# Expert layers with a table of tokens by slot, and feed-forward stages with routed tiles between halves of the shared expert

## The reference, cut to what matters

```python
# L0_ffn: 8 experts, two per token, inner width 512
probs = softmax(30 * tanh((x @ w_gate) / 30)); mask = one_hot(top_k(probs, 2)).sum(-2)
out = sum_e (silu(x @ w1[e]) * (x @ w3[e])) @ w2[e] * (probs * mask)[:, e]
# L1_ffn, second part: 8 routed experts of width 176, two per token, and a shared one of width 704
h = rms(x) * w_ln2;  probs = softmax(h @ w_router);  combine = the two largest probs, 0 elsewhere
routed = sum_e combine[:, e] * (silu(h @ w_gate_e[e]) * (h @ w_up_e[e])) @ w_down_e[e]
sh = (silu(h @ w_sh_gate) * (h @ w_sh_up)) @ w_sh_down * sigmoid(h @ w_sh_eg)
x = x + routed + sh
```

## Time and profile before

| | |
|---|---|
| Time, median of 3 runs | 2636.81 us (2633.54 to 2636.89) |
| Profiled execution | 2635.1 us, its span 2633.0 us |
| Instructions | 45240 |
| PE busy | 2078.7 us (79%), mean granted clock 0.857 |
| DVE, ACT, POOL busy | 1525.1 (58%), 1180.3 (45%), 1044.7 us (40%) |
| DMA | 179.47 MB, mean 68 GB/s |

### The profile page before, as it was taken

How to read it: one execution, slowest core, us unless ns; L and a number is a source line. 1 busy time by engine, 2 the same in 40 slices (tenths; PEclk the granted TensorE clock), 3 DMA queues, 4 the chain that set the end, 5 groups by cost and what they waited for, 6 DMA issues and landing times. The chain is left out here.

```text
span 2633.0 us, 45240 instructions
## 1 busy us (share of the span) xinstructions
PE 2078.7 (79%) x16876; PEld 1605.9 (61%) x16888; DVE 1525.1 (58%) x3266; ACT 1180.3 (45%) x2905; POOL 1044.7 (40%) x965
## 2 busy tenths in 40 slices
PE   8497438978887995967798577976789676779798
PEld 5365225646565874756587466865668665546686
DVE  2222642236675335787876876868778678357432
ACT  3211421126364333853566545655556555236433
POOL 0222012220002542586535864368623767100254
PEclk9698768989998997967799588996789777989799
DMA  8422013210003303321322213222122221120430
GB/s 288 132 24 48 9 39 71 25 44 2 23 2 97 142 0 70 106 73 33 113 80 78 69 50 100 89 63 81 57 89 81 67 69 65 37 55 2 126 113 16
DMA packets 138317, 179.47 MB, mean 68 GB/s; under 512 B 62048, under 2 KB 114544, under 8 KB 132992
## 3 DMA queue, kind: packets, MB, share of 16 engines
q1 hardware_dynamic: 129952, 166.46, 20.4%
q0 software_dynamic: 8160, 10.26, 2.5%
HBM read 154.52 MB, written 22.17 MB: 67 GB/s over the span
## 5 line engine op out<-in xcount | busy, mean ns | idle before, releaser
L2695 DVE SCALAR_TENSOR_TENSOR XT<-M_delta,CW_delta,XT 128x256 f32<-128x256 f32 x576 | 249.0, 495 | 67.7 <-ACT M_delta L2475 39.7
L2146 PE MATMUL PS<-XP_delta,X 128*128 128x268 f32 (+1 forms) x1024 | 247.2, 395 | 19.8 <-DMA X<-in_L_attn_b_heads 15.6
L2146 PEld LDWEIGHTS PS<-XP_delta,X 128*128 128x128 f32 x1024 | 196.0, 193 | 71.8 <-DMA X<-in_L_attn_b_heads 19.8
L1541 PE MATMUL PS<-XP_rffn,UW_rffn 128*128 128x512 f32 x816 | 195.3, 396 | 4.6 <-POOL UW_rffn L1495 4.6
L1541 PEld LDWEIGHTS PS<-XP_rffn,UW_rffn 128*128 128x128 f32 x816 | 156.4, 192 | 38.4 <-issue 5.4
L1273 ACT ACTIVATE PR_attn<-PS,NM_attn 128x256 f32<-128x256 f32 (+1 forms) x384 | 130.8, 448 | 103.5 <-DVE NM_attn L1343 103.5
L1495 POOL TENSOR_TENSOR UW_rffn<-W_rffn,UW_rffn 128x512 fp32r<-128x512 f32 x34 | 43.7, 1286 | 301.5 <-ACT UW_rffn L1602 301.5
L561 POOL DMA_INDIRECT sums<-XS_moe,token_moe x46 | 71.7, 1559 | 221.4 <-ACT XS_moe L661 207.0
L2613 ACT ACTIVATE S_delta<-S_delta,AO_delta 128x128 f32<-128x128 f32 x512 | 159.5, 393 | 0.0
L1663 DVE TENSOR_TENSOR SU_rffn<-PS,CB_rffn 128x512 f32<-128x512 f32 x68 | 47.0, 691 | 179.4 <-PE PS L1541 157.0
L2177 PE MATMUL PS<-KQ_delta,TR_delta 128*128 128x64 f32 x1024 | 133.8, 275 | 9.6 <-ACT TR_delta L2540 8.4
(11 more groups left out here) (459 smaller groups left out, 5259.5 us busy)
## 6 DMA issues: line engine op xcount, KB each, us to landing
M_delta<-gram_delta SPq DMA_DIRECT2D x32, 1280.0 KB, 6.0
X<-in_L_attn_b_heads SPq DMA_DIRECT2D x64, 512.0 KB, 3.5
EW<-in_L_ffn_w SPq DMA_DIRECT2D x24, 512.0 KB, 10.0
CB_rffn<-routes_rffn SPq DMA_DIRECT2D x20, 512.0 KB, 21.9
XN<-in_L_attn_b_outs SPq DMA_DIRECT2D x16, 512.0 KB, 3.7
F_delta<-in_L_attn_b_outs SPq DMA_DIRECT2D x4, 2048.0 KB, 9.5
W_rffn<-in_L_ffn_tiles SPq DMA_DIRECT2D x4, 1536.0 KB, 11.5
slots<-pad SPq DMA_DIRECT2D x2, 2967.0 KB, 14.1
```

Of the source, the lines that this page charges most:

```text
L1541: last = nc.tensor.matmul(PS[:, 4 + 2 * n + q, :], UW[qw][:, r, (q * KD + k) * P:(q * KD + k + 1) * P], XP[qx][:, k, n * NB:(n + 1) * NB], ...
L2146: last = nc.tensor.matmul(PS[:, 1 + i, 0:B * (WIN - halo)], WH[:, r, i, k, :], XP[:, k, :, n * BT + halo:n * BT + WIN], start=(k == 0), st ...
L2695: nc.vector.scalar_tensor_tensor(TMP[:, r, i], RAW[:, r, i, :, tau:tau + BT], CW[:, i, h, tau:tau + 1], TMP[:, r, i], ALU.mult, ALU.add).t ...
```

## The change

`moe`: the tensor `slots`, its fills, the copies into `XW`, the scatters and the read-back are gone. DVE builds a one-hot matrix `spread` of each choice's lane in its tile, and `entries`, which hold for each choice, in the column of its tile, the token (relative to a constant for empty slots) and the weight. 16 matmuls of PE sum up a table `token[lane, tile]`, `share[lane, tile]`. SP writes the normed rows to the DRAM tensor `rows`; POOL gathers each tile of slots from there by indirect DMA, six tiles ahead. PE's order is `ranks`, `experts` (the 23 register loads), `table`. The tile loop is as before.

`routed_ffn`: only the shared expert (6 column tiles) is computed for all tokens, in two halves of 512 tokens; between them 23 tiles of slots go through their routed expert in plain fp32, with weights `EWR` in SBUF. SP writes each answer tile to DRAM; when all have landed, POOL gathers them, two per token tile, and DVE adds them with the routing weight, among the products of half 1. PE's order is: `up(0,0)`, the router, `up` and `down` of half 0 with `ranks` and `table` among them, `experts`, the routed tiles, half 1. Weights are split once. A common class `Routing` serves both.

The diff, cut (`...` for what is left out):

```diff
+class Routing:
...
+    def ranks(self, pe):
+        nc, PS = self.core.nc, self.core.PS
+        pe.wait_ge(self.consts, 2)
+        pe.wait_ge(self.pick_d, 1)
+        m = self.picked[:].rearrange("p i e -> p (i e)")
+        nc.tensor.matmul(PS[:, 6, 0:NT * E], self.ones[:], m, start=True, stop=True).then_inc(self.sum_mm, 1)
+        at = lambda i: PS[:, 7, P + i * E:P + NT * E]
+        nc.tensor.matmul(at(0), self.before[:], m, start=True, stop=False)
+        for i in range(1, NT):
+            last = nc.tensor.matmul(at(i), self.ones[:], m[:, 0:(NT - i) * E], start=False, stop=i == NT - 1)
+        last.then_inc(self.sum_mm, 1)
+    def table(self, pe, spread):
+        nc, PS = self.core.nc, self.core.PS
+        w = (1 + self.weighted) * self.TILES
+        pe.wait_ge(self.entry_d, 1)
+        for j in range(2 * NT):
+            pe.wait_ge(self.spread_d, j // NT + 1)
+            last = nc.tensor.matmul(PS[:, 6, P:P + w], spread[:, j], self.entry[:, j].rearrange("p x t -> p (x t)"),
+                                    start=j == 0, stop=j == 2 * NT - 1)
+        last.then_inc(self.table_mm, 1)
+    def experts(self, pe):
+        pe.wait_ge(self.owner_d, 1)
+        return [pe.value_load(self.owner[0:1, t:t + 1], min_val=0, max_val=E - 1) for t in range(self.TILES)]
...
+    def place(self, dve, c):
...
+        c.then(nc.vector.tensor_tensor(self.at_least, by_slot(self.where).broadcast_to([P, 2 * NT, t + 1]),
+                                       self.tile_at[:].unsqueeze(1).broadcast_to([P, 2 * NT, t + 1]), ALU.is_ge))
+        c.then(nc.vector.tensor_reduce(self.tiles_up[:], self.at_least, AX.X, ALU.add))
+        c.then(nc.vector.scalar_tensor_tensor(self.lo[:], self.tiles_up[:], -float(P), self.where[:], ALU.mult, ALU.add))
+    def spread(self, dve, spread, half):
+        nc = self.core.nc
+        h = slice(half * NT, (half + 1) * NT)
+        nc.vector.tensor_tensor(spread[:, h], self.lane[:].unsqueeze(1).broadcast_to([P, NT, P]),
+                                self.lo[:, h].unsqueeze(2).broadcast_to([P, NT, P]), ALU.is_equal).then_inc(self.spread_d, 1)
+    def entries(self, dve, c):
+        nc, t = self.core.nc, self.TILES
+        over = lambda x: x.unsqueeze(2).broadcast_to([P, 2 * NT, t])
+        nc.vector.scalar_tensor_tensor(self.value[:].rearrange("p (r i) -> p r i", r=2), self.lo[:].rearrange("p (r i) -> p r i", r=2),
+                                       -1.0, self.row[:].unsqueeze(1).broadcast_to([P, 2, NT]), ALU.mult, ALU.add)
+        c.then(nc.vector.tensor_tensor(self.in_tile, self.at_least[:, :, 0:t], self.at_least[:, :, 1:t + 1], ALU.subtract))
+        last = nc.vector.tensor_tensor(self.entry[:, :, 0], self.in_tile, over(self.value[:]), ALU.mult)
+        if self.weighted:
+            last = nc.vector.tensor_tensor(self.entry[:, :, 1], self.in_tile,
+                                           over(self.weight[:].rearrange("p r i -> p (r i)")), ALU.mult)
+        last.then_inc(self.entry_d, 1)
...
+    def tokens(self, dve, c):
+        nc, PS, t = self.core.nc, self.core.PS, self.TILES
+        dve.wait_ge(self.table_mm, 1)
+        if self.weighted:
+            nc.vector.tensor_copy(self.share[:], PS[:, 6, P + t:P + 2 * t])
+        c.then(nc.vector.tensor_tensor(self.token_f[:], PS[:, 6, P:P + t], self.own[:].broadcast_to([P, t]), ALU.add))
+        nc.vector.tensor_copy(self.token[:], self.token_f[:]).then_inc(self.token_d, 1)
...
 def moe(core, a="L0_ffn_"):
...
+            norm.rows_ready(sp)
+            sp.dma_start(rows, XN[:]).then_inc(rows_out, 16)
...
+            def gather(t):
+                nc.gpsimd.indirect_dma_start(XS[:, t], None, core.rows[:],
+                                             bass.IndirectOffsetOnAxis(ap=token[:, t:t + 1], axis=0)).then_inc(x_in[t], 16)
+            routing.constants(pool)
+            pool.wait_ge(core.zeroed, 32)
+            pool.wait_ge(rows_out, 16)
+            pool.wait_ge(routing.token_d, 1)
+            for t in range(AHEAD):
+                gather(t)
             pool.wait_ge(base_out, 16)
             for t in range(TILES):
                 pool.wait_ge(y_ev, t + 1)
                 if t or layer_no:
                     pool.wait_ge(added, 16 * (TILES * layer_no + t))
                 nc.gpsimd.indirect_dma_start(core.sums[:], bass.IndirectOffsetOnAxis(ap=token[:, t:t + 1], axis=0),
+                                             XS[:, t], None, compute_op=ALU.add).then_inc(added, 16)
+                if t + AHEAD < TILES:
+                    gather(t + AHEAD)
...
+            routing.ranks(pe)
+            e = routing.experts(pe)
+            routing.table(pe, spread)
             pe.wait_ge(core.expert_in, 48 * E)
...
+            routing.place(dve, c)
+            routing.spread(dve, spread, 0)
+            routing.entries(dve, c)
+            routing.spread(dve, spread, 1)
+            routing.owners(dve, c)
+            routing.tokens(dve, c)
...
 def routed_ffn(core):
...
+            sp.dma_start(EWR[:], a["L1_ffn_experts"]).then_inc(experts_in, 16)
+            for t in range(TILES):
+                sp.wait_ge(y_ev, t + 1)
+                sp.dma_start(answers[t * P:(t + 1) * P], XS[:, t]).then_inc(y_out, 16)
...
+            routing.constants(pool)
+            up_low(0)
+            up_low(1)
+            down_low(0)
+            up_low(2)
+            for m in range(ST - 1):
+                hidden_low(m)
+                if m + 1 < ST:
+                    down_low(m + 1)
+                if m + 3 < ST:
+                    up_low(m + 3)
+            pool.wait_ge(rows_out, 16)
+            pool.wait_ge(routing.token_d, 1)
+            for t in range(3):
+                gather(t)
+            hidden_low(ST - 1)
+            for t in range(3, TILES):
+                gather(t)
             nc.gpsimd.tensor_tensor(X[:], X[:], XN[:], ALU.add).then_inc(res_d, 1)
+            pool.wait_ge(routing.slot_d, 1)
+            pool.wait_ge(y_out, 16 * TILES)
+            for i in range(NT):
+                for r in range(2):
+                    nc.gpsimd.indirect_dma_start(
+                        G[:, r, i], None, answers,
+                        bass.IndirectOffsetOnAxis(ap=routing.slot[:, r, i:i + 1], axis=0)).then_inc(returned[i], 16)
...
             norm.tensor(pe)
             norm.ready(pe)
+            up(0, 0)
...
+            up(0, 1)
+            up(0, 2)
+            down(0, 0)
+            pe.wait_ge(log_d, 1)
+            routing.ranks(pe)
+            up(0, 3)
+            down(0, 1)
+            up(0, 4)
+            down(0, 2)
+            up(0, 5)
+            routing.table(pe, spread)
+            down(0, 3)
+            down(0, 4)
+            down(0, 5)
+            e = routing.experts(pe)
+            pe.wait_ge(h_d, ST)
+            pe.wait_ge(experts_in, 16)
+            pe.wait_ge(routing.token_d, 1)
+            for t in range(3):
+                turn(t)
+            pe.wait_ge(yt_ev, KD)
+            for t in range(TILES):
+                gate_up(t)
+                if t >= 1:
+                    turn_hidden(t - 1)
+                if t + 3 < TILES:
+                    turn(t + 3)
+                if t >= 2:
+                    answer(t - 2)
+            turn_hidden(TILES - 1)
+            answer(TILES - 2)
+            answer(TILES - 1)
+            up(1, 0)
+            pe.wait_ge(xk_d, TILES)
+            shared_rows(0, 6)
+            up(1, 1)
+            up(1, 2)
+            for m in range(ST):
+                down(1, m)
+                if m + 3 < ST:
+                    up(1, m + 3)
+            pe.wait_ge(h_d, 2 * ST)
+            shared_rows(1, 2)
...
+            routing.choose(dve, c, prob)
+            product(1)
+            product(2)
+            routing.place(dve, c)
+            routing.entries(dve, c)
+            product(3)
+            routing.spread(dve, spread, 0)
+            product(4)
+            routing.spread(dve, spread, 1)
+            nc.vector.tensor_copy(routing.slot[:].rearrange("p r i -> p (r i)"), routing.where[:]).then_inc(routing.slot_d, 1)
+            routing.owners(dve, c)
+            product(5)
+            routing.tokens(dve, c)
...
```

726 lines of the change are left out of this document (380 added, 346 removed).

## The result

In the comparison that answers to the forecast the changed kernel took 2668.0 us (median of 4 runs, 2659.4 to 2672.9) against 2635.2 (4 runs): ratio **1.0126**, 95% interval 1.0109 to 1.0144. The forecast was 2627.2, range 2604 to 2647: wrong in size and in sign. The same code, run again beside the kernel before in two later series of runs, gave 0.9994 (0.998 to 1.0008) and 1.0000 (0.9981 to 1.0019), at 2631.1 and 2630.5 us. So the change is worth nothing, and in the first series it cost 1.3%. The three other executions of that first comparison, 2659.4 to 2672.4 us, are as long as the profiled one, so its trace stands for all four. Both numbers need an explanation, and both can be read from the stages.

What follows compares the result with a forecast made beforehand. TensorE (PE) was taken to bound the tile loops of both stages. +14.6 us for two expert layers and -24.2 for two feed-forward stages gave -9.6: 2625.5 for the profiled execution, 2627.2 for the median, range 2604 to 2647.

Steps and rivals of the forecast that it cites:

- Expert layer, +7.3 a layer: In `moe`, first transpose at 113.9 instead of 106.6, the table waiting behind the register loads: +7.3 us a layer, +14.6 for two.
- Half 0 of the shared expert to `down(0,5)`: In `routed_ffn`, 108 matmuls (24.5 us) plus routing, waits and 3 us of POOL contention: `down(0,5)` at 868.2, stage starting at 814.2.
- Register loads exposed: In `routed_ffn`, the 23 register loads behind `down(0,5)` hold up everything later in PE's queue: 15.3 us.
- the register loads are hidden after all: Rival, both stages: loads cost nothing; -8.0 in each `moe`, -26.4 in each feed-forward stage, 2568 us; chance 0.04.
- Tiles at 2.47 us: In `routed_ffn`, each of the 23 routed tiles takes PE 2.47 us, 56.8 in all, DVE and ACT staying well below.
- rival of slow tiles: Rival, `routed_ffn` tile loop: routed tiles don't keep 2.47 us; at 2.9 it costs 20 us, 2647 us; chance 0.14.
- half 0 at the low clock: Rival, `routed_ffn`: PE's waits keep half 0 slow, up to 20 us a stage; half of that gives 2647; chance 0.09.
- From the first routed turn to the last answer: In `routed_ffn`, 56.8 us of tiles plus 0.6 first turns, 3.5 low clock and 2 for the last chain, ending at 946.7.
- Half 1 and the end: In `routed_ffn`, 24.5 us of matmuls, 0.9 transposes, 1 stalls: last `down` ends at 973.1, stage at 977.8, -12.1 a stage.
- The gathers and the 5 MB of expert weights hide behind it: In `routed_ffn`, the gathers and expert weights cost no time of their own, hidden behind the 15.3 us of register loads.
- just hidden: In `routed_ffn`, POOL's 16 returning gathers (20.3 us plus 3 to land) end at 973.1, beside half 1; slow gathers cost some 7.
- the rest is not edited: All stages but two `moe` and two `routed_ffn` (741 of 2633 us) stay unedited apart from set-up lines; no time change allowed.

Runs made afterwards that it cites:

- r1: The changed kernel run once more, unedited, for a second trace in a later series: 2631.1 us, ratio 0.9994 to the kernel before.
- r9: Changed kernel with the table ahead of the register loads and those loads made inside the tile loops of both stages, gathers in a row: 2564.3 us, ratio 0.9739.
- r12: The changed kernel repeated unedited in another later series, to meet the state with late signals: 2630.5 us, ratio 1.0000 to the kernel before.
- r2: Only the expert layers changed, feed-forward stages those of the kernel before: 2645.3 us, ratio 1.0059.
- r6: The kernel before plus 87 idle instructions in PE's queue in the delta stage, giving it the changed kernel's place in the instruction stream: ratio 1.0027.
- r5: The changed kernel plus 169 idle instructions in PE's queue in the delta stage, restoring its old place in the instruction stream: ratio 1.0147.

## Why the prediction was wrong

- *Expert layer, +7.3 a layer:* right in sum (+7.0 and +6.4 in r1) and step by step, with the table "directly behind the last register load". The first layer of the first trace had 3.8 more; its router products ran at the low clock, 6.97 us where the earlier trace rows has 4.22 (2.75 of it).
- *Half 0 of the shared expert to `down(0,5)`:* 54.0 forecast, 53.7 measured, including the 3 us for POOL and DVE in each other's way (the owners' cast took 0.77 us in r1, 0.18 in the expert layer). The first `up` came 1.1 us later than forecast, so the single terms are not as good as their sum.
- *Register loads exposed:* right, "a hole of about 15 us in PE". The rival "the register loads are hidden after all" is refuted for this order, and r9 shows what it would have been worth once the loads are moved: 14.3 a stage.
- *Tiles at 2.47 us:* right, 2.48. The rival of slow tiles fell, and so did that of half 0 at the low clock: its granted clock in r1 is 0.87 (840 to 852 us), 1.00 (to 864) and 0.83 (to 884).
- *From the first routed turn to the last answer:* 62.9 forecast, 60.7 in r1. The 6.1 us allowed beside the tiles for the low clock, the first turns and the last chain were some 3.7.
- *Half 1 and the end:* 31.1 forecast, 30.7 in r1; the returning gathers are hidden as forecast. Against the old stage of other traces (171.6 to 171.9) the gain is 11.4 a stage, against the earlier trace rows 15.5 and 13.7.
- **The step that failed first: the price of the gathers in the feed-forward stage.** "The gathers and the 5 MB of expert weights hide behind it" for the row of 23, and "just hidden" for the 16 that return: the walk had each as 1.3 us of POOL and nothing more. In the first comparison they came with 16.9 us a stage of late completions, 33.8 us in all. Why the signals are late stays open. I had no row of PE at work beside a row of gathers: in the earlier trace rows POOL issues 16 scatters while PE does nothing. I gave the transfers no term for what they do to other engines' signals.
- **The step that failed second: "the rest is not edited".** Code behind an edit is moved by it. The delta stage was 12.6 (r1), 16.1 (first trace) and 6.4 us (r12) longer; some 7 of it is the place of its bursts in PE's stream. The remainder differs from trace to trace and lies mostly at the stage's start and in its first block: its first write of `beta_delta` comes 33 us behind the start against 29, in r2, with the old feed-forward stage, as well. Of these 4 us, 2.5 are two groups of products, 6.98 and 6.17 us in r1 against 5.45 and 5.15 before; r6, whose code is that of before up to there, has 6.98 and 6.34. So this part also comes without an edit, and is not explained by one.
- *Sum:* forecast -9.6. In r1: +13.4 (layers), -29.2 (feed-forward), +12.6 (delta), -2.4 (others) = -5.6 of span. The medians of that series differ by 0.3 us only: the old feed-forward stage of the earlier trace rows was 2 to 4 us longer than in r2, so less was gained on average than from that one trace. That the median of r1 lies inside the forecast's range is therefore luck in part: a gain larger than forecast in the feed-forward stages covers a delta stage that had no term. First trace: +17.2, +4.6, +16.1, +0.2 = +38.1.

## What to carry to other kernels

A register load on an engine that is the bound cost its full price here only where it stood in a row ahead of work; one per tile, two or three tiles ahead, it was free (66.8 us of 2631 together with the order of the table). After an edit that changes the number of instructions, compare the stages that you did not touch, block by block, before you believe a difference under 1%: a burst of short instructions is sensitive to where it is cut, and an extra cut may take the clock with it. And take a trace of the changed kernel more than once, in more than one series: two traces of the same code differed here by 44 us, 34 of them late signals in four places.

## What the runs showed of the hardware that I had not expected

- A burst that issues some 65 products a microsecond (158 in 2.43 us) stops 1.2 to 2.5 us at a boundary of 256 instructions, and twice when two boundaries lie in it or at its end; in the third block the granted clock then was 0.83 over 16 us instead of 1.00.
- A completion of PE may reach ACT 6.9 us late while POOL issues indirect gathers back to back (1.25 us apart), in some series of runs and not in others of the same chip; gathers 5.8 us apart in the same traces keep all their completion records, those in a row lose most of them.
- Register loads are taken by PE's sequencer while its array works: with the table ahead, first turn 10.7 us earlier for 7.0 us of matmuls moved.
- A wait that is already met is not free on PE: 168 of the 169 idle ones are on record in r5, from 1055.63 to 1073.70, so 0.11 us each, and PE's next product came 14 us later although PE seemed to have time there.
